# Cross-attention and a two-expert feed-forward layer: five places reordered, four normalisations on ScalarE, epsilon on POOL

## The reference

```python
q = layernorm(x)                      # over the last axis, eps 1e-5
qh, kh, vh = 8 heads of 16 rows each of q, ctx, ctx
sm = softmax(einsum('bhdq,bhdl->bhql', qh, kh) / sqrt(16))
x = x + gamma * einsum('bhql,bhdl->bhdq', sm, vh)
xn = layernorm(x)
top = argmax(softmax(xn @ Wg.T))      # two experts
out0 = gelu(xn @ W0a.T + b0a) @ W0b.T + b0b
out1 = relu(xn @ W1a.T + b1a) @ W1b.T + b1b
x = x + where(top == 0, out0, out1)
```

## Time and profile before

| | |
|---|---|
| median of 3 runs | 233.16 us (233.03 to 233.47) |
| the profiled execution | 232.91 us, its span 231.1 us |
| PE busy | 217.1 us (94%), 2036 instructions |
| PEld busy | 165.9 us (72%) |
| DVE busy | 174.3 us (75%) |
| ACT busy | 145.6 us (63%) |
| POOL busy | 137.8 us (60%) |
| granted TensorE clock | 1.00 throughout |

### The profile page before, as it was taken

How to read it: one execution, slowest core, us unless ns; L and a number is a source line. 1 busy time by engine, 2 the same in 40 slices (tenths; PEclk the granted TensorE clock), 3 DMA queues, 4 the chain that set the end, 5 groups by cost and what they waited for, 6 DMA issues and landing times.

```text
span 231.1 us, 5325 instructions
## 1 busy us (share of the span) xinstructions
PE 217.1 (94%) x2036; PEld 165.9 (72%) x2041; DVE 174.3 (75%) x357; ACT 145.6 (63%) x220; POOL 137.8 (60%) x180
## 2 busy tenths in 40 slices
PE   7789879788999999999999999999999999899995
PEld 3334445456787978788787978797879787778995
DVE  7499977999579976997699869994888444545583
ACT  6205766856985597658784779477944986624240
POOL 6852314879889718972698358934762287382800
PEclk9999999999999999999999999999999999999999
DMA  4785499543224340625052704250302000000101
GB/s 136 244 301 185 140 372 375 176 142 139 92 85 150 113 143 16 240 67 191 4 198 74 237 1 119 94 180 33 72 1 72 0 27 3 23 26 0 47 3 45
DMA packets 19393, 26.40 MB, mean 114 GB/s; under 512 B 1992, under 2 KB 12840, under 8 KB 19112
## 3 DMA queue, kind: packets, MB, share of 16 engines
q1 hardware_dynamic: 18942, 25.66, 33.4%
q10 hardware_dynamic: 426, 0.40, 0.5%
HBM read 11.01 MB, written 2.10 MB: 57 GB/s over the span
## 4 chain that ended last, share of the span: by engine, by line
PE 76%; DVE 8%; ACT 5%; DMA 4%; issue 3%; SPq 3%; POOL 1%
PE ff L775 20%; PE ff L795 12%; PE od L722 11%; PE st L710 10%; PE ff L807 7%; PE smax L697 5%; DVE nmax L396 3%; PE od L730 3%; DMA qkst<-mlow 2%; PE od L737 2%; PE tr L748 2%; ACT P L576 2%; PE tr L758 2%; DMA qkst<-parts 1%; PE od L679 1%
## 5 line engine op out<-in xcount | busy, mean ns | idle before, releaser
L576 ACT ACTIVATE P<-st 128x1024 f32<-128x1024 f32 x64 | 66.1, 1033 | 47.7 <-PE st L710 47.3
L396 DVE TENSOR_REDUCE nmax<-smax 128x4 f32<-128x1024 f32 x56 | 68.5, 1224 | 21.3 <-PE smax L697 20.5
L267 POOL TENSOR_TENSOR mv<-mv,power 128x1 f32<-128x1 f32 x32 | 19.1, 596 | 47.9 <-DVE mv L378 47.8
L775 PE MATMUL ff<-xnTh,w1h 128*128 128x256 f32 x128 | 38.1, 298 | 1.0 <-DVE y L495 1.0
L775 PE MATMUL ff<-xnTl,w1h 128*128 128x256 f32 x128 | 36.0, 281 | 0.0
L775 PE MATMUL ff<-xnTh,w1l 128*128 128x256 f32 x128 | 35.9, 281 | 0.0
L285 POOL TENSOR_TENSOR hidL<-hid,hidH 128x1024 fp32r<-128x1024 f32 x13 | 31.0, 2386 | 6.0 <-DVE hidH L457 4.6
L609 ACT ACTIVATE hid<-ff,b1t 128x256 f32<-128x256 f32 x64 | 26.1, 479 | 12.2 <-PE ff L775 12.1
L710 PE MATMUL st<-qkst 64*128 64x256 f32 x256 | 32.2, 330 | 1.4 <-ACT P L576 0.5
L795 PE MATMUL ff<-w2h,hidH 128*128 128x256 f32 x124 | 32.1, 292 | 0.0
L722 PE MATMUL od<-P,vt 128*32 128x256 f32 x512 | 30.9, 382 | 0.0
(11 more groups left out here) (81 smaller groups left out, 369.6 us busy)
## 6 DMA issues: line engine op xcount, KB each, us to landing
qkst<-parts SPq DMA_DIRECT2D x47, 256.0 KB
xv<-in_xv SPq DMA_DIRECT2D x16, 256.0 KB, 3.0
qk<-in_qk SPq DMA_DIRECT2D x15, 256.0 KB, 3.1
out<-y SPq DMA_DIRECT2D x16, 128.0 KB, 2.7
w1t<-in_w SPq DMA_DIRECT2D x1, 1024.0 KB, 7.2
w2t<-in_w SPq DMA_DIRECT2D x1, 1024.0 KB, 7.9
qkst<-parts ACTq DMA_DIRECT2D x1, 256.0 KB
qkst<-mlow SPq DMA_DIRECT2D x16, 8.0 KB
```

The lines of the kernel that those rows point to most:

```text
L267: pool.tensor_tensor(mv[:, b % 2, 11:12], mv[:, b % 2, 10:11], power[:, 0:1], ALU.pow).then_inc(s_rstd, 1)
L396: dve.tensor_reduce(nmax[:, c % 2, :, :, j].rearrange("p a e -> p e a"), (ff if c in WIDE and j % 2 else smax)[:, :, :, :], AX.X, ALU.max, ...
L576: act.activation(P[:, b % 2, j, :, :, :].rearrange("p e a l -> p (e a l)"), st[:, :, :, :].rearrange("p e a l -> p (e a l)"), ACT.Exp, sca ...
L775: mm = pe.matmul(ff[:, u // 2 % 2, u % 2, :], w[:, a, e, m * 128:(m + 1) * 128], xs[:, i % 2, a, :], start=a == 0 and n == 0, stop=a == LC ...
```

## The change

Two things at once.

The reordering: WIDE takes in batch 4. The high parts of the weights are made two slots later, and behind the slot's other ScalarE work. gemm1's units 0 and 1 go ahead of transpose_att in j=0, with 2 and 3 behind it; in even batches from 4 on transpose_x moves from j=2 to j=3, behind the slot's scores and maxima. In odd batches high_xT (ScalarE) goes ahead of the exp of j=3 and low_xT (VectorE) ahead of the reduce. In the tails values(B-1) goes between gemm1's units 1 and 2, copy_od(B-1) between the same units of hidden, and x_norm(B-1) ahead of low_relu.

The statistics: VectorE no longer adds epsilon; POOL does, for all 32, ahead of the power. For q of batches 6 and 7 (ACT_Q) and for the sums of batches 0 and 1 (ACT_X) POOL also makes the offset, minus mean times the power, by two more instructions, and ScalarE normalises by Identity with that bias and the power as scale: q in slots 10 and 14, x in slots 9 and 13. The gate of batches 0 and 1 moves from j=1 to j=2. New waits keep the statistics' two places in mv1 and mv2 from being overwritten before ScalarE has read them.

```diff
-WIDE = range(0, 4)
+WIDE = range(0, 5)
+
+ACT_Q = range(6, 8)
+ACT_X = range(0, 2)
...
-            def rstd(b, mv, count, s_var, s_rstd):
-                pool.wait_ge(s_var, count)
+            def rstd(b, mv, s_var, s_eps, s_rstd):
+                pool.wait_ge(s_var, b + 1)
+                pool.tensor_scalar(mv[:, b % 2, 10:11], mv[:, b % 2, 9:10], EPS, None, ALU.add).then_inc(s_eps, 1)
+                pool.wait_ge(s_eps, b + 1)
                 pool.tensor_tensor(mv[:, b % 2, 11:12], mv[:, b % 2, 10:11], power[:, 0:1], ALU.pow).then_inc(s_rstd, 1)
+
+            def offset(m, count, s_neg, s_off):
+
+                pool.tensor_scalar(m[:, 12:13], m[:, 8:9], -1.0, None, ALU.mult).then_inc(s_neg, 1)
+                pool.wait_ge(s_neg, count)
+                pool.tensor_tensor(m[:, 13:14], m[:, 12:13], m[:, 11:12], ALU.mult).then_inc(s_off, 1)
+
+            def rstd1(c):
+                rstd(c, mv1, s_var1, s_eps1, s_rstd1)
+                if c in ACT_Q:
+                    pool.wait_ge(s_rstd1, c + 1)
+                    offset(mv1[:, c % 2, :], c - ACT_Q.start + 1, s_neg1, s_off1)
...
-                dve.bn_aggr(m[:, 8:10], m[:, 0:6]).then_inc(s_aggr, 1)
-                dve.wait_ge(s_aggr, count)
-                dve.tensor_scalar_add(m[:, 10:11], m[:, 9:10], EPS).then_inc(s_var, 1)
+                dve.bn_aggr(m[:, 8:10], m[:, 0:6]).then_inc(s_var, 1)
...
@@ vector, the loop @@
+                if j == 3 and b >= 2 and b % 2:
+                    low_xT(b - 2)
                 if c < B:
                     take_max(c, k)
...
                 for p in prepared(n - 1):
-                    q_norm(p)
+                    if p not in ACT_Q:
+                        q_norm(p)
...
-                if j == 1 and b >= 2:
+                if j == 1 and b >= 2 and b - 2 not in ACT_X:
                     x_norm(b - 2)
+                    gate(b - 2)
+                if j == 2 and b - 2 in ACT_X:
                     gate(b - 2)
...
+            x_norm(B - 1)
             low_relu(LAST - 1)
-            x_norm(B - 1)
...
@@ scalar @@
+            def act_norm(out, src, m, s_done):
+                act.activation(out, src, ACT.Identity, bias=m[:, 13:14], scale=m[:, 11:12]).then_inc(s_done, 1)
...
+                if j == 3 and b >= 2 and b % 2:
+                    high_xT(b - 2)
                 if b >= 0:
                     exp(b, j)
...
-                if n in (6, 7):
...
-                if n in (10, 11):
...
+                if n in (8, 9):
...
+                if n in (12, 13):
...
+                if j == 1 and b - 2 in ACT_X:
+                    x_norm(b - 2)
                 if j == 2 and b >= 1:
                     copy_od(b - 1)
...
+                for p in prepared(n - 1):
+                    if p in ACT_Q:
+                        q_norm(p)
...
-            for u in range(4):
+            for u in range(0, 2):
                 hidden(LAST - 1, u)
             copy_od(B - 1)
+            for u in range(2, 4):
+                hidden(LAST - 1, u)
...
@@ tensor @@
                 if j == 0:
+                    if even:
+                        for u in range(0, 2):
+                            gemm1((b - 4) // 2, u)
                     if b >= 2:
                         transpose_att(b - 2)
                     if even:
-                        for u in range(0, 4):
+                        for u in range(2, 4):
                             gemm1((b - 4) // 2, u)
...
-                    if b >= 2:
+                    if b >= 2 and not even:
                         transpose_x(b - 2, min(b + 2, B))
                 if j == 3 and b >= 1:
+                    if even:
+                        transpose_x(b - 2, min(b + 2, B))
...
-            for u in range(0, 4):
+            for u in range(0, 2):
                 gemm1(B // 2 - 2, u)
             values(B - 1)
+            for u in range(2, 4):
+                gemm1(B // 2 - 2, u)
```

More of the change, by code:

```diff
@@ L264, in _, with rstd2 @@
         def _(pool):
-            def rstd(b, mv, count, s_var, s_rstd):
-                pool.wait_ge(s_var, count)
+            def rstd(b, mv, s_var, s_eps, s_rstd):
+                pool.wait_ge(s_var, b + 1)
+                pool.tensor_scalar(mv[:, b % 2, 10:11], mv[:, b % 2, 9:10], EPS, None, ALU.add).then_inc(s_eps, 1)
+                pool.wait_ge(s_eps, b + 1)
                 pool.tensor_tensor(mv[:, b % 2, 11:12], mv[:, b % 2, 10:11], power[:, 0:1], ALU.pow).then_inc(s_rstd, 1)
+            def offset(m, count, s_neg, s_off):
[7 more added lines that the diff above has]
+                    offset(mv1[:, c % 2, :], c - ACT_Q.start + 1, s_neg1, s_off1)
+            def rstd2(b):
+                rstd(b, mv2, s_var2, s_eps2, s_rstd2)
+                if b in ACT_X:
+                    pool.wait_ge(s_rstd2, b + 1)
+                    offset(mv2[:, b % 2, :], b - ACT_X.start + 1, s_neg2, s_off2)
             def low(c):
@@ L311, in _ @@
             pool.wait_ge(s_const, 1)
-            rstd(0, mv1, 1, s_var1, s_rstd1)
-            rstd(1, mv1, 2, s_var1, s_rstd1)
+            rstd1(0)
+            rstd1(1)
             pool.wait_ge(s_k0hi, 1)
@@ L530, in _ @@
                     normalise(b - 1)
-                    if b >= 2:
+                    if b >= 2 and b % 2 == 0:
                         low_xT(b - 2)
@@ L570, in high, with q_norm, x_norm @@
                 act.activation(parts[:, c % 2, 1:3, :], qk[:, place(c, QK), :, :], ACT.Copy).then_inc(s_hi, 1)
+            def act_norm(out, src, m, s_done):
+                act.activation(out, src, ACT.Identity, bias=m[:, 13:14], scale=m[:, 11:12]).then_inc(s_done, 1)
+            def q_norm(c):
+                act.wait_ge(s_off1, c - ACT_Q.start + 1)
+                if c == ACT_Q.start:
+                    act.wait_ge(s_qn, c)
+                act_norm(qk[:, place(c, QK), 0, :], qk[:, place(c, QK), 0, :], mv1[:, c % 2, :], s_qn)
+            def x_norm(b):
+                act.wait_ge(s_off2, b - ACT_X.start + 1)
+                act_norm(xn[:, b % 2, :], x1[:, b % X1, :], mv2[:, b % 2, :], s_xn)
             def exp(b, j):
@@ L642, in _ @@
                     row_copy(act, 0, 0)
-                if n in (6, 7):
-                    act.wait_ge(s_w1, 16)
-                    act.activation(w1h[:, n - 6, :, :], w1t[:, n - 6, :, :], ACT.Copy).then_inc(s_w1h, 1)
-                if n in (10, 11):
-                    act.wait_ge(s_w2, 16)
-                    half = slice((n - 10) * HM, (n - 9) * HM)
-                    act.activation(w2h[:, half, :], w2t[:, half, :], ACT.Copy).then_inc(s_w2h, 1)
                 for p in prepared(n - 2 if n > 0 else n - 1) if n else ():
@@ L653, in _ @@
                     copy_max(c - 1)
+                if n in (8, 9):
+                    act.wait_ge(s_w1, 16)
+                    half = n - 8
+                    act.activation(w1h[:, half, :, :], w1t[:, half, :, :], ACT.Copy).then_inc(s_w1h, 1)
+                if n in (12, 13):
+                    act.wait_ge(s_w2, 16)
+                    half = slice((n - 12) * HM, (n - 11) * HM)
+                    act.activation(w2h[:, half, :], w2t[:, half, :], ACT.Copy).then_inc(s_w2h, 1)
+                if j == 1 and b - 2 in ACT_X:
+                    x_norm(b - 2)
                 if j == 2 and b >= 1:
@@ L658, in _ @@
                             hidden((b - 4) // 2, u)
-                if j == 3 and b >= 2:
+                for p in prepared(n - 1):
+                    if p in ACT_Q:
+                        q_norm(p)
+                if j == 3 and b >= 2 and b % 2 == 0:
                     high_xT(b - 2)
-                    if b >= 4 and b % 2 == 0:
+                    if b >= 4:
                         high_relu((b - 4) // 2)
-            for u in range(4):
+            for u in range(0, 2):
                 hidden(LAST - 1, u)
             copy_od(B - 1)
+            for u in range(2, 4):
+                hidden(LAST - 1, u)
             high_xT(B - 2)
```

30 lines of the change are left out of this document (19 added, 11 removed).

## The result

The change takes 230.86 us (median of 6 runs, 230.66 to 231.92), the kernel before 233.03 beside it (232.78 to 233.47): a ratio of 0.9917, 95% interval [0.9895, 0.994]. The forecast was 230.2, its range 228.8 to 231.9. The profiled execution took 230.66 us, its span 228.9.

What follows compares the result with a forecast made beforehand. TensorE was taken as bound, idle only at 35.7 to 56.2 and 199.7 to 216.8 us. Terms -0.1 (to slot 16), -0.5 and -2.4 sum to -3.0: 229.9 from the profiled 232.91, 230.2 as median; range 228.8 to 231.9.

Steps and rivals of the forecast that it cites:

- Start: Before the first maxima: epsilon on POOL instead of VectorE delays the low parts' DMA, +0.2 us (bounds 0 and +0.6).
- Slots 5 to 8: Passes 5 to 8 over n: the ods stall goes, but slot 8 still waits for the mlow row; gain 0.
- Slots 8 to 16: Passes 8 to 16 over n: VectorE is relieved, POOL's statistics chain becomes the pacer; -0.3 us.
- Double batches: About 56 to 200 us: moving transpose_x removes its wait for mlow, but hidL limits the gain; -0.5 us.
- Tail: Last slots: three TensorE stalls (y of batch 11, ods, transpose of x 15) go; -2.4 us.
- A: Rival, double batches: hidL doesn't bind, each gains 0.26, so -0.8 us more, 229.4 us; chance 0.14.
- B: Rival, early slots: the stalls vanish as POOL isn't the pacer, -1.5 us or so more, 228.7 us; chance 0.12.
- C: Rival: POOL's product costs as much as the power, or the tail's tight places miss; +1.3, 231.5 us; chance 0.18.
- D: Rival, early slots: each small POOL instruction costs what the power does, slot 16 comes 4.1 later; 234.3 us; chance 0.04.
- E: Rival, ScalarE: Identity isn't in the loaded table, eight loads at 1.28 us; above 237 us; chance 0.02.
- F: Rival, tail: nothing moves because the last y's wait elsewhere; 232.6 us; chance 0.04.

Runs made afterwards that it cites:

- order_g1_back: The reordering without the moved statistics (order_only), with gemm1 of the double batches undivided again behind transpose_att: 228.76 us, ratio 0.9817 to the kernel before.
- no_act_norm: The change with all normalisations back on VectorE, epsilon still on POOL: 229.41 us, ratio 0.9837 to the kernel before.
- tail_back: The change with the old order of the last slots: 233.36 us, ratio 1.0027 to the kernel before.
- order_only: The change with the statistics as before (epsilon and all normalisations on VectorE), so the reordering alone: 228.72 us, ratio 0.9837 to the kernel before.
- eps_dve: The change with epsilon on VectorE again, the four normalisations still on ScalarE: 229.18 us, ratio 0.9845 to the kernel before.
- after_spin: The change with 8 instead of 3 filler matmuls in slot 11: 231.42 us, ratio 0.9929 to the kernel before.
- order_spin5: The reordering alone (order_only) with 5 instead of 3 filler matmuls in slot 11: 229.74 us, ratio 0.9869 to the kernel before.

## Why the prediction was right or wrong

**Start (+0.2): mechanism right, delay not seen.** The powers come 0.3 later (5.24 for 4.93), but the low parts' DMA landed in 2.80 us where before had 3.11, and the first maxima came at 10.14 for 10.09. That is luck of a transfer. Slot 0 lies at 19.32 to 19.68 over all fourteen traces (before 19.44, the change 19.47).

**Slots 5 to 8 (0): right.** The ods stall went, and slot 8 started when the mlow row landed, 5.12 us after its issue where before had 5.56. No edit reaches that difference: where the other traces show it, it is 5.08 to 5.93.

**Slots 8 to 16 (-0.3, -0.1 with the start; measured +0.12): the pacer was right, two sizes were off.** POOL's chain is as forecast (0.22, 0.57, 0.24 and 0.19; product forecast 0.25), slot 12 came at 44.69 for 44.7, and both exponentials stand where they were put. The normalisation on ScalarE took 0.60 for 0.40, taken from a Copy of that size. And the walk ended at 54.8 where slot 16 came at 55.12, 0.3 late; the forecast had the chain of q 7 end at 53.0 and it ended at 52.97, but ScalarE took the normalisation up only at 53.18, behind exponentials that the fallen clock had made late, and the normalisation was 0.2 longer than laid down. The forecast said nothing of the clock; in the change the fall costs 0.1 at slot 16 and nothing in the end. It also compared against the earlier trace rows only, not against the new order without the statistics: order_g1_back reaches slot 16 at 54.27 (the others without the moved statistics at 53.92 to 54.84), so the statistics cost about 0.8 here.

**Double batches (-0.5; measured +0.17): the failed step.** "POOL's added epsilons (0.3 each) fall into its idle time (0.92 before 140.12)". The idle time is there, but the epsilon stands ahead of POOL's sums, and the sums end beside q, which then takes 0.54 for 0.39. This pushes hidH and hidL by 0.15, in just those four batches where the prediction itself had found hidL to bind. Cost 0.6 (no_act_norm). The other parts held, and closely: from slot 24 to 60 the order alone gives -0.5 (109.63 for 110.15), 0.08 in each stretch of eight slots where hidL binds (24.28 for 24.36) and 0.28 in batch 12 (13.07 for 13.35). hidL binds in batches 4 to 10 (0.8 in four waits), the wait at L807's successor L865 was called, and the split of gemm1 costs its 0.03 to 0.04 a batch from slot 24 on, though over slots 16 to 60 nothing is left of it (order_g1_back).

**Tail (-2.4): right**, -2.5 by the places and by tail_back's median, -2.25 by tail_back's places, each of the three stalls for its own reason.

**Rivals.** A (hidL doesn't bind) is refuted by the waits of order_only. B is half true of the reordering alone: in order_g1_back slot 16 comes 0.7 earlier, but one wait for nmax (0.66) stays and the one for xnTl is longer (1.62 for 0.87). C's number (231.5) is as near to what happened as the forecast's, but by another cause: the product is cheap (0.19) and the tail's places all held. D and E are refuted: small POOL instructions cost 0.19 to 0.31 on average, and no table is loaded beside Identity. F is refuted by the tail.

So the sum came out 0.7 too low, within the range, because the statistics were priced by their durations and not by what stands behind them. It was partly luck that the total lay so near: the fall of TensorE's clock, which the forecast did not have, happened to be taken up by POOL's queue here.

What stays open: how much of the interaction between epsilon and normalisations (2.1 together, 0.5 and 0.7 apart, so about 1.0 from their meeting) is POOL's queue before slot 16 and how much is the first hidL at 70 us. The two places show 0.66 and 0.44, which together would cover it: against eps_dve, after_spin is 0.66 behind at slot 16, 1.15 at slot 24 and 1.62 at slot 60, where the last 0.47 is epsilon's price in batches 6 to 10. But after_spin has eight fillers besides, and no run separates the two places.

## What to carry to other kernels

Price a small instruction by the queue behind it: 0.22 us ahead of POOL's sums cost 0.15 us in each double batch where hidL binds, through a VectorE instruction that ran into them. Take a bundle apart before judging it: here a reordering worth 4.1 us carried statistics that gave 2.1 of it back. An instruction that seems late in an order may stand there to keep clear of another engine; look at what it would run beside before moving it.

## What the runs showed of the hardware

- Some VectorE instructions from SBUF to SBUF that start beside a POOL tensor_tensor end only about when it does: q took 2.59 us for 0.39 beside hidL. The statistics of x (0.43) and instructions that read PSUM (attT, 0.42) are not held. In the change gate_prod took 1.32 us for 0.43 beside w2l (52.93 to 54.21):

```profile
53.16 1.32 DVE L474 CUSTOM_DVE_ANT_0 gate_prod<-xn,wgd 128x256 f32<-128x256 f32 x1
```

- POOL on 128x1, on average: tensor_scalar 0.227 us (epsilon), tensor_tensor 0.192, a power 0.589.
- ScalarE's Identity with a scale and a bias per partition took 0.60 us on 128x256, a Copy of that size 0.40 (L619).
- TensorE's granted clock fell to 0.50 for about 3 us after gaps of 1.2 and 0.5 us (the change), or of 1.6 us (order_only), and not after a gap of 1.6 us in order_g1_back's profiled execution; in order_only an execution with the fall is 1.2 to 2.0 us longer.
- The landing of one 8 KB row (mlow, ahead of slot 8) took 5.08 us (order_spin5) to 5.93 us (no_act_norm) from the end of its issue, and moved the start of slot 8 with it.
